# A vision tower of edge filters, attention and a sign layer: another order for the first five images and for the last steps, with constant products in TensorE's waits

## The reference

```python
gray = einsum('bchw,c->bhw', x, (0.2989, 0.587, 0.114))
edges = conv3x3(gray, scharr)                  # 2 filters, zero padding
h = sqrt(square(edges)).sum(axis=1) / 2
n = layernorm(h)
c_q, c_kv = n @ W_dq, n @ W_dkv                # 256 -> 64
Q, K, V = c_q @ W_uq, c_kv @ W_uk, c_kv @ W_uv # 64 -> 16 heads x 16
y = h + softmax(causal(Q K^T / 4)) V @ W_o
z = y + layernorm(y) @ sign(weight)^T
```

## Time and profile before

| | |
|---|---|
| time, median of 3 runs | 435.55 us (433.94 to 436.83) |
| time of the profiled execution | 436.89 us |
| its span | 435.1 us |
| busy: PE, DVE, ACT, POOL | 368.5, 288.9, 238.9, 172.0 us |
| DMA | 74.13 MB, 170 GB/s over the span |

### The profile page before, as it was taken

The page is one execution under the profiler, slowest core; times in us unless marked ns, Lnnn a source line. Parts: engine busy times, 40 slices in busy tenths (PEclk is TensorE's granted clock), DMA queues, the critical chain, the costliest instruction groups (busy, mean ns, idle before and its releaser), DMA issues.

```text
span 435.1 us, 9881 instructions
## 1 busy us (share of the span) xinstructions
PE 368.5 (85%) x3545; PEld 261.5 (60%) x3588; DVE 288.9 (66%) x539; ACT 238.9 (55%) x408; POOL 172.0 (40%) x367
## 2 busy tenths in 40 slices
PE   0335686999999999999999999999999989796764
PEld 0122364666676767676767676767676757574442
DVE  2224176886868687868686868686878776775520
ACT  2123425666767676767676767676757563534301
POOL 7032022545554546454545454545434323212200
PEclk9998669799999999999999999999999989898975
DMA  5966797959596878787878787675753534200000
GB/s 173 226 157 149 181 257 203 269 171 257 174 245 187 230 209 220 208 223 202 219 202 223 202 224 201 199 210 160 203 151 102 145 108 132 88 27 1 26 24 24
DMA packets 72266, 74.13 MB, mean 170 GB/s; under 512 B 6387, under 2 KB 66075, under 8 KB 72219
## 3 DMA queue, kind: packets, MB, share of 16 engines
q1 hardware_dynamic: 71355, 73.11, 61.5%
q10 hardware_dynamic: 864, 0.39, 0.3%
HBM read 51.98 MB, written 21.04 MB: 168 GB/s over the span
## 4 chain that ended last, share of the span: by engine, by line
PE 75%; DMA 7%; issue 5%; ACT 5%; DVE 4%; SPq 1%; POOL 1%; ACTq 0%; POOLq 0%
PE bank L910 14%; PE bank L1034 8%; PE bank L971 7%; PE bank L921 7%; PE bank L998 6%; PE bank L947 4%; PE bank L937 4%; PE bank L903 4%; PE bank L956 3%; PE bank L973 3%; PE bank L1037 3%; PE bank L1000 3%; PE bank L1015 3%; PE bank L984 3%; DMA q_st<-top_rows 3%
## 5 line engine op out<-in xcount | busy, mean ns | idle before, releaser
L628 ACT ACTIVATE probs<-bank 128x1024 f32<-128x1024 f32 x64 | 65.2, 1018 | 50.9 <-PE bank L1000 50.2
L774 DVE TENSOR_REDUCE top<-bank 128x4 f32<-128x1024 f32 x64 | 78.0, 1219 | 19.6 <-PE bank L973 19.5
L784 DVE TENSOR_TENSOR bank<-bank,cap_kq 128x512 f32<-128x512 f32 x64 | 44.7, 698 | 23.0 <-PE bank L1015 21.6
L971 PE MATMUL bank<-k_st,q_st 96*128 96x256 bf16 x256 | 48.3, 283 | 2.8 <-DMA k_st<-qk_parts 2.8
L921 PE MATMUL bank<-rows,band 102*32 102x256 f32 x512 | 34.1, 411 | 17.4 <-DMA rows<-gray_padded 17.4
L998 PE MATMUL bank<-q_st,k_st 99*128 99x256 bf16 x256 | 47.3, 278 | 1.0 <-DMA q_st<-top_rows 0.8
L1034 PE MATMUL bank<-probs,v_ring 128*32 128x256 f32 x512 | 42.4, 403 | 3.9 <-DVE rest L761 1.9
L779 DVE TENSOR_REDUCE top<-bank 128x4 f32<-128x512 f32 x64 | 41.6, 649 | 0.0
L471 POOL TENSOR_SCALAR var<-mv 128x2 f32<-128x2 f32 x16 | 3.6, 227 | 95.2 <-DVE mv L816 95.2
L633 ACT ACTIVATE probs<-bank 128x512 f32<-128x512 f32 x64 | 38.0, 594 | 3.8 <-DVE bank L784 3.6
L791 DVE STREAM_TRANSPOSE u<-bank 128x256 f32<-128x256 f32 x64 | 28.7, 448 | 11.1 <-PE bank L1037 5.9
(11 more groups left out here) (97 smaller groups left out, 750.9 us busy)
## 6 DMA issues: line engine op xcount, KB each, us to landing
x_sb<-in_x SPq DMA_DIRECT2D x16, 768.0 KB, 6.0
rows<-gray_padded SPq DMA_DIRECT2D x48, 256.0 KB
qk_parts<-parts SPq DMA_DIRECT2D x48, 256.0 KB, 3.1
q_st<-qk_parts SPq DMA_DIRECT2D x96, 128.0 KB, 3.0
k_st<-qk_parts SPq DMA_DIRECT2D x96, 128.0 KB, 3.0
gray_padded<-gray SPq DMA_DIRECT2D x16, 258.0 KB, 3.1
out_dram<-z SPq DMA_DIRECT2D x16, 256.0 KB, 3.0
rows<-gray_padded SPq DMA_DIRECT2D x32, 24.0 KB
```

Of the source, the lines that this page charges most:

```text
L628: nc.scalar.activation(probs[:, g, :, 0:S], ps_k0, ACT.Exp, scale=SCALE).then_inc(exp0_done, 1)
L774: nc.vector.tensor_reduce(top[:, 1, g // 2, :, g % 2], ps_hi, AX.X, ALU.max, negate=True).then_inc(max_hi_done, 1)
L784: nc.vector.tensor_tensor(ps_k1, ps_k1, cap_kq[:, :].unsqueeze(1).to_broadcast([P, G, P]), ALU.min).then_inc(capped, 1)
L971: nc.tensor.matmul(ps_hi[:, i, :], q[:, hh, P:S], k[:, hh, :], start=(i == b * two), stop=False, skip_group_check=True)
```

## The change

- SP's list at the start is written out anew: operands of image 0 are loaded right behind its parts, ahead of the rows of images 2 and 3; `load_x(4)` and `load_x(5)` stand behind the operands of image 1 and ahead of those of image 2, `load_x(6)` behind these. `load_operands` waits for the third part only at its third pair of transfers. The projections' weights and the ones rows go to ACT's queue.
- For images 0 and 1 DVE adds the edges and makes variance and shift itself, POOL only takes the root (`sum_and_scale`, `root_x`); second and third parts are made in halves.
- ACT and DVE have written-out lists for images 0 and 1 in place of iterations -4 to -1. `turn_x(2)`, `compress(2)` and `expand_qk(2)` move from iteration 0 to 1, `filters(2)` from -1 to 0 (into banks 3 and 4), `turn_max(0, 0)` ahead of the third group, `values(0, 0)` behind the second group of image 1; the signs move from iteration 1 to 2.
- `keep_warm(count)` puts products of constants into bank 5, whose result nobody reads: 36 ahead of the first filters, 10 each behind `filters(0)`, behind `expand_v(0)` and in iteration 0, then 5 and 8 in iteration 17.
- At the end `measure_y` comes right behind `add_y` for images 13 to 15, `turn_y` of these has a bank of its own (0), and in iteration 17 `project(15)`, in banks of its own, comes ahead of `feed_forward(14)`. `add_y`, `add_z` and `store_z` of image 15 go by halves of the rows.

```diff
-        sp.wait_ge(third_out[n % 2], 16 * (n // 2 + 1))
...
         for j in range(len(FROM_Q)):
+            if j == 2:
+                sp.wait_ge(third_out[n % 2], 16 * (n // 2 + 1))
...
+        if n == IMAGES - 1:
+            for t in range(T):
+                sp.wait_ge(z_done if t else top_z_done, n + 1 if t else 1)
+                sp.dma_start(out[n, t * P:(t + 1) * P, :], z[:, n % 2, t, :]).then_inc(z_out[n % 2], 16)
+            return
...
@@ -348,23 +366,9 @@
...
-    def load_projections():
...
@@ -372,49 +376,51 @@
...
-    for i in range(FIRST, LAST + 1):
-        if i == -4:
-            store_gray(0)
-            load_rows(0)
-            load_projections()
-            store_gray(1)
-            load_x(2)
-            load_rows(1)
-            load_x(3)
-            set_ones()
-        if i == -3:
-            store_gray(2)
-            load_rows(2)
-        if i == -2:
-            store_parts(0)
-            store_third(0)
-            store_gray(3)
-            load_rows(3)
-            load_operands(0, 0)
-            load_operands(0, 1)
...
-            if i == 0:
-                load_x(4)
-            elif live(i + 5):
-                load_x(i + 5)
-            if live(i + 1):
-                load_operands(i + 1, 0)
-                load_operands(i + 1, 1)
-            if i == 0:
-                load_outputs()
-            if live(i + 4):
-                store_gray(i + 4)
-            if i == 0:
-                load_x(5)
-            if live(i - 3):
-                store_z(i - 3)
-            if live(i + 4):
-                load_rows(i + 4)
...
+    store_gray(0)
+    load_rows(0)
+    store_gray(1)
+    load_x(2)
+    load_rows(1)
+    load_x(3)
+    store_gray(2)
+    store_gray(3)
+    store_parts(0)
+    store_third(0)
+    load_operands(0, 0)
+    load_rows(2)
+    load_operands(0, 1)
+    load_rows(3)
+    store_parts(1)
+    store_third(1)
+    load_operands(1, 0)
+    load_operands(1, 1)
+    load_x(4)
+    load_x(5)
+    load_outputs()
+    for i in range(1, LAST + 1):
+        if live(i + 1):
+            store_parts(i + 1)
+        if i == 1:
+            store_gray(4)
+        if live(i + 1):
+            store_third(i + 1)
+        if i == 1:
+            load_rows(4)
+        elif live(i + 5):
+            load_x(i + 5)
+        if live(i + 1):
+            load_operands(i + 1, 0)
+            load_operands(i + 1, 1)
+        if i == 1:
+            load_x(6)
+        if live(i + 4):
+            store_gray(i + 4)
+        if live(i - 3):
+            store_z(i - 3)
+        if live(i + 4):
+            load_rows(i + 4)
+    sp.wait_ge(z_out[0], 16 * IMAGES // 2)
+    sp.wait_ge(z_out[1], 16 * (IMAGES // 2 + 1))
...
@@ -454,6 +460,10 @@
...
+    def root_x(n):
+        pool.wait_ge(var_done, n + 1)
+        pool.tensor_tensor(rstd[:, :], var[:, :], power[:, :], ALU.pow).then_inc(rstd_done, 1)
...
@@ -535,10 +545,14 @@
...
+    for i in range(LAST + 1):
         if live(i - 1):
...
         if live(i + 2):
             sum_edges(i + 2)
...
-        if live(i):
+        if live(i) and i:
...
@@ -560,6 +574,20 @@
...
+    def load_projections():
...
@@ -642,55 +676,85 @@
...
+    first_gray(0)
+    first_gray(1)
+    load_projections()
+    set_ones()
+    both_edges(0)
+    normalize_x(0)
+    first_gray(2)
+    copy_xt(0)
+    copy_c(0)
+    first_gray(3)
+    first_part(0)
+    second_part_halves(0)
+    both_edges(1)
+    copy_v(0)
+    normalize_x(1)
+    copy_xt(1)
+    copy_c(1)
+    first_part(1)
+    second_part_halves(1)
+    for i in range(LAST + 1):
...
+        if i == 1:
+            copy_xt(2)
+            copy_c(2)
+        elif live(i + 1) and i:
             second_part(i + 1)
...
+        if live(i + 1) and i != 1:
             copy_v(i + 1)
-        if live(i + 2):
+        if i == 0:
+            both_edges(2)
+        if i == 0:
+            copy_max_rows(0, 0)
+        if live(i + 2) and i != 1:
             normalize_x(i + 2)
         if live(i - 1):
...
+        if i == 1:
+            first_part(2)
+            first_gray(4)
+            second_part(2)
+            copy_v(2)
+            normalize_x(3)
+        if live(i + 4) and i > 1:
             scale_colors(i + 4)
-        if live(i + 2):
+        if live(i + 2) and i > 1:
...
+        if i == 1:
+            copy_xt(3)
+            scale_colors(5)
+        if live(i + 2) and i:
             copy_c(i + 2)
-        if live(i):
+        if live(i) and i:
             copy_max_rows(i, 0)
...
+        if live(i + 2) and i:
             first_part(i + 2)
...
-        if i in (-3, -2, 0):
-            first_gray(i + 5 if i < 0 else 4)
...
@@ -754,6 +818,30 @@
...
+    def sum_and_scale(n):
+        for t in range(T):
+            dve.wait_ge(abs_done, T * n + t + 1)
+            nc.vector.tensor_tensor(h_ring[:, n % H_RING, t, :], edge[:, t, 0, :], edge[:, t, 1, :],
+                                    ALU.add).then_inc(h_done if t else top_h_done, 1)
+            dve.wait_ge(h_done if t else top_h_done, n + 1)
+            nc.vector.bn_stats(stats[:, t, :], h_ring[:, n % H_RING, t, :]).then_inc(stats_done, 1)
+        need(dve, xn_done, T * n)
+        for t in range(T):
+            dve.wait_ge(stats_done, T * n + t + 1)
+            nc.vector.bn_aggr(mv[:, t, :], stats[:, t, :]).then_inc(mv_done, 1)
+        dve.wait_ge(mv_done, T * (n + 1))
+        nc.vector.tensor_scalar(var[:, :], mv[:, :, 1], EPS, None, ALU.add).then_inc(var_done, 1)
+        dve.wait_ge(rstd_done, n + 1)
+        nc.vector.scalar_tensor_tensor(shift[:, :], mv[:, :, 0], -1.0, rstd[:, :],
+                                       ALU.mult, ALU.mult).then_inc(shift_done, 1)
...
+    def third_part_halves(n):
+        for k, i in enumerate((1, 0)):
+            dve.wait_ge(part1_done if k else key_part1_done, n + 1)
...
@@ -816,26 +907,38 @@
...
     nc.vector.memset(first[:, :], 0.0).then_inc(warmed, 1)
-    for i in range(FIRST, LAST + 1):
-        if i == FIRST:
-            rest_of_gray(0)
-            rest_of_gray(1)
-            make_band()
-        if live(i + 1):
+    rest_of_gray(0)
+    rest_of_gray(1)
+    make_band()
+    make_up()
+    sum_and_scale(0)
+    rest_of_gray(2)
+    rest_of_gray(3)
+    rest_of_parts(0)
+    third_part_halves(0)
+    sum_and_scale(1)
+    rest_of_parts(1)
+    third_part_halves(1)
+    for i in range(LAST + 1):
+        if live(i + 1) and i > 1:
             rest_of_parts(i + 1)
-            if i + 1 < ON_VECTOR:
...
+        if live(i + 2) and i > 1:
             measure_h(i + 2)
...
-        if i == -3:
-            make_up()
-        if i in (-2, -1):
-            rest_of_gray(i + 4)
...
         if i == 1:
-            make_signs()
-        if live(i - 1):
-            cap(i - 1, 1)
-        if live(i - 1):
+            measure_h(3)
+            rest_of_parts(2)
...
             turn_values(i - 1, 0)
         if live(i):
             max_hi(i, 1)
             max_lo(i, 1)
+        if i == 1:
+            turn_values(0, 0)
+            rest_of_gray(4)
         if live(i - 2):
...
-        if i == 1:
-            copy_signs()
+        if i == 2:
+            make_signs()
+        if i == LAST - 1:
+            add_y(i - 2)
+            measure_y(i - 2)
...
@@ -870,27 +976,31 @@
...
+        if i == 0:
+            measure_h(2)
+        if i == 2:
+            copy_signs()
...
+        if live(i - 2) and i < LAST - 1:
             add_y(i - 2)
+            if i >= LAST - 3:
+                measure_y(i - 2)
         if live(i - 1):
...
+        if live(i - 2) and i < LAST - 3:
             measure_y(i - 2)
...
-        if i == 0:
-            rest_of_gray(4)
...
         last.then_inc(done, 1)
...
@@ -1068,44 +1194,75 @@
...
+        if n >= IMAGES - 2:
+            pe.wait_ge(z_done, n)
...
+    def keep_warm(count):
+        for _ in range(count):
+            nc.tensor.matmul(bank[:, 5, :], ident_bf[:, :], mask_qk[:, :, :], start=True, stop=True)
     pe.wait_ge(drawn, 2 * TAPS + 5)
+    keep_warm(36)
...
+        if i == 1:
+            pe.wait_ge(ones_in, ST_RING * 16)
...
+        if i == 1:
+            turn_x(2)
...
-        if i == 0:
-            pe.wait_ge(ones_in, ST_RING * 16)
...
+            compress(2)
         if live(i - 1):
...
+        if live(i + 1) and i not in (0, 1):
             expand_v(i + 1)
+        if i == -1:
+            keep_warm(10)
+        if i == 0:
+            keep_warm(10)
...
+        if i == 1:
+            expand_qk(2)
+        elif live(i - 1):
             values(i - 1, 0)
...
+        if i == 1:
+            values(0, 0)
+            expand_v(2)
+        if i == 0:
+            expand_v(1)
+            filters(2)
+            turn_max(0, 0)
+        if live(i + 2) and i not in (0, 1):
             turn_x(i + 2)
-        if i == 1:
-            pe.wait_ge(signed, 1)
-            pe.wait_ge(v_copied, 3)
-            turn(ps_w, signs, turned)
+        if i == LAST - 1:
+            keep_warm(5)
+            project(i - 2)
         if live(i - 3):
```

(44 more changed lines are left out.)

124 lines of the change are left out of this document (78 added, 46 removed).

## The result

The changed kernel takes 418.86 us in the median of 4 runs (417.42 to 420.82), the kernel before 434.75 in its 4: a ratio of 0.9633, 95% interval 0.9569 to 0.9697, some 16 us. 411.5 was predicted, with 405 to 421 as the range. The profiled execution took 420.82 at a span of 419.0, so it compares with 436.89 and 435.1.

The account below looks back on a forecast made before the run. TensorE bounds the middle, so only the two ends can gain, the start being held by an order of transfers. 436.9 - 11.9 (start) - 12.3 (end) = 412.7, stated as 411.5 against the median; range 405 to 421.

Parts of the forecast that it names:

- The forecast of the start: Everything up to iteration 2: scores 13.3 us earlier, +0.9 in iteration 0, 0 in iteration 1, +0.5 for signs: -11.9 us.
- DMA sets the start: Rival: landings stretch by 2 us at three places in a row, giving back 5 to 8 us: 417 to 420, chance 0.14.
- growing landings: Sign against the forecast: it would be wrong if DMA landings grow in the new trace.
- The end, 12.3: Iterations 16 and 17: -3.2 and -9.1 us, the latter bounded by -9.5 and 0; projection of image 15 starts earlier.
- Constant products, 36: Ahead of the first filters: end at 18.4, filters then take 1.93 not 3.68; net -0.7 us, bounds -2.0 and +4.2.
- Layernorm by DVE: Image 0, end of filters to transposes: 4.0 us instead of 6.6, so -2.6, bounds -3.2 and -1.
- The clock behind them, -2.5: Image 0's transposes, compress and expand run faster behind the constant products: 0.66, 1.03 and 1.04 us; bounds 0 and -2.5.
- Parts and operands, -2.9 and "scores at 42.6": Image 0: parts 2.9 us shorter, done at 32.2; first operand load at 34.7, not 47.97; scores at 42.6, 13.3 earlier.
- Iteration 0, +0.9: From the first scores to the first key scores: 14.4 us against 13.5, bounds -1 and +3.
- Iteration 1, 0 with a bound of +4: Wait of 3.93 and half speed go, a new chain comes in: 23.8 us, no gain; bounds -4.9 and +4.
- Steady state: Images in the middle: 21.7 us each between 130 and 340, no faster than before.
- The 1% for warming up: Skill's figure for the clock's warm-up: clock terms at both ends at most about 4.4 us, not 7.4; result about 415.

Follow-up runs that it names:

- e2: Changed kernel with the end of before (images 13 to 15, no constant products there), so the start alone: ratio 0.9943 to the kernel before.
- e1: Kernel before with only the changes of the end (images 13 to 15, with its 5 and 8 constant products): ratio 0.9681 to the kernel before.
- e4: Changed kernel without the 5 and 8 constant products of the end: ratio 0.9650 to the kernel before.
- e5: Changed kernel with the grey picture of image 3 behind the parts of image 0: ratio 0.9626 to the kernel before.
- e11: Changed kernel with rows of image 3 behind the parts of image 1 and the grey picture of image 4 earlier: ratio 0.9659 to the kernel before.
- e8: Changed kernel with 20 instead of 10 constant products behind the filters of image 0: ratio 0.9624 to the kernel before.
- e9: Changed kernel with the projections' weights back on SP's queue, behind the rows of image 0: ratio 0.9635 to the kernel before.
- e12: Changed kernel with 3.1 MB fewer loaded for x of images 3 to 5 and rows of 3 and 4, same order: ratio 0.9514 to the kernel before.
- e3: Changed kernel without any of the 79 constant products: ratio 0.9770 to the kernel before.
- e6: Changed kernel with the rows of image 3 loaded behind the stores of the parts of image 1: ratio 0.9600 to the kernel before.

## Why the prediction was right, and where its size was off

The direction, the range and the end were right. The forecast of the start was not: of 11.9 us came 2.5 (e2). The rival "DMA sets the start" (417 to 420, chance 0.14) is what came, and the prediction's own sign of being wrong, growing landings, came too. That 418.9 lies within the range is because the range took in that rival.

- *The end, 12.3*: measured 13.9 as e1's ratio, 14.0 in e1's trace, 12.8 in the changed kernel's from the transposes of image 12 on (58.5 us before, 45.7 after), with its 1.4 us of late stores. `project(15)` came 3.05 behind the last values (3.6 forecast), and from its start to the end of the last product it is 9.1, as forecast. The constants' part is 1.5 us by e4's trace, far from the 9.5 us between the bounds of this iteration.
- *Constant products, 36*: to end at 18.4, ended at 18.34; filters of 1.93 as said.
- *Layernorm by DVE*: 4.3 us for 4.0 forecast and 6.6 before.
- *The clock behind them, -2.5*: this step failed in its size. Ten products fill 2.3 of 4.3 us, and the clock fell inside `compress` (1.68, then 2.08 and 3.37): 0.5 for the transposes, 0.4 for `compress`, the rest nothing. Whether it falls there differs from execution to execution (it didn't in e5 and e11). e8 pays the whole term, and the time stays.
- *Parts and operands, -2.9 and "scores at 42.6"*: the scores came at 45.1. The first operand load was issued at 39.03, 4.3 later than forecast: 2.0 of that are clock and layernorm (`expand_qk` ended at 30.4 for 28.4), the rest the parts behind x of image 3. I had x landing at 26 to 28.5; it landed at 31.7, 10.5 us after its issue, where the trace of before has 6.9. With the weights on SP's queue it took 6.9 again (e9), and the prediction has no term for the move of the weights. By luck 1.8 us came back: from the first operand load to the scores it took 6.1, not 7.9, since the last of the six landed in 2.8 and not in 4.63.
- *Iteration 0, +0.9*: +2.0 (15.5 for 13.5).
- *Iteration 1, 0 with a bound of +4*: it was +5.7 (29.4 for 23.7), the largest miss. The step that failed is the landing of the parts of image 1 (7.12, where the prediction has some 3 for a store), the wait of 3.0 that follows, and half speed behind it up to 71; the waits of 1.4, 1.2 and 1.1 add to it. With fewer bytes the iteration took 23.3 (e12).
- *Steady state*: 21.7 an image, as said. The start's gain shrank further there, from 3.2 at the filters of image 4 to 1.9 at those of image 15, by pauses of 0.4 and 1.1 us in two images; with the same start e2 and e4, and with nearly the same e9, kept 4.6 to 6.0. So one execution's trace is good to some 4 us at that place.
- *The 1% for warming up*, which the prediction took from the Trainium skill ("TensorE: Matmul & The Clock Gate", section "Part 1: The HAM clock gate"), would have given an estimated 415 and was nearer to the result, but for another reason. The constants are worth some 6 us here by e3, in intervals too wide to tell that from its 4.4. What was missing was transfers, not clock.

## What to carry to other kernels

When a start is made denser, cost its transfers by what stands ahead of them in the queue and not by the landing times of the old list. Here SP issued 3.2 MB between 39.0 and 51.3 us ahead of the parts of image 1 (twelve operand loads of 128 KB, and rows of two images of 0.8 MB each), while 2.5 MB were moved (205 GB/s); before, it was 2.4 MB issued and 2.1 moved in 10.4 us. By these numbers an estimated 0.7 MB stood ahead where it had been 0.3, and the second store took 7.1 us where it had taken 3.2. The rate over the stretch doesn't tell: before had 248 GB/s where these stores landed in 3.2. Small loads moved to a second queue aren't free either: by e9's trace they cost x of images 2 and 3 some 2 us each here. Taking the wait at the head of such a list away shows the next one; an experiment that moves fewer bytes in the same order tells in one run whether the engines' steps or the transfers are the limit. At an end without transfers, putting the longest chain first, with what goes with it, was worth 14 us, and filler work only some 1.5 of them.

## What the runs showed of the hardware

- DMA: the second of three stores of parts (256 KB each) landed in 2.9 us from its issue on a queue that had gone quiet, and in 6.1 to 7.8 in the nine traces with 1.6 MB issued in the 6 us ahead of it. With the rows of image 3 (0.8 MB) behind the store it took 4.5 and 4.7 (e6, e11).
- DMA: 768 KB of x of images 2 and 3 took 5.4 and 6.9 us before, 5.5 and 6.9 in e9, and 10.6 to 12.1 and 8.0 to 10.5 in the traces with 320 KB of weights on ACT's queue at that time.
- TensorE: 36 products of constants from a cold start took 10.23 us, and 9.3 to 10.8 over the ten traces that have them; at the higher speed it would be an estimated 7.9 (36 of 0.22). Behind ten constants and a wait of 1.99 us `compress` took 1.10 in two traces and 1.49 to 2.05 in six.
- TensorE: a wait of 0.8 us before the projection of image 15, behind others of 1.3 and 0.6 us, was followed by half speed in most of it (3.52, e4); with five constants in the last of them it took 1.89.
- The granted clock at the start (0.91 before over 55.9 us) doesn't show the half speed that the lengths of the first filters show (3.64 against 1.93).
